# A two-layer graph network on one core: key one-hots on VectorE alone, elu read from PSUM, key sums by a block of ones

## The chip, the cores and the metric

The kernel runs on one core of one Trainium2 chip. The metric is the device time of one execution in microseconds. A core has TensorE (PE in the profile), VectorE (DVE), ScalarE (ACT), GpSimd (POOL) and SyncE (SP, which only issues transfers here). They run their own instruction streams and meet at semaphores.

## The reference, cut to what matters

Two layers on 1250 nodes of 512 features with 21250 weighted edges (`src`, `dst` sorted, `edge_weight`).

```python
xn = layernorm(x)
x = x + gcn(xn, edges, ew, W, b) + linear_attention(xn, w_qkv, w_out, b_out)
x = x + ffn0(layernorm(x))
xn = layernorm(x)
x = x + relu(segment_sum(((xn @ U * s) @ Vt)[dst] * ew, src) + bias) + softmax_attention(xn, w_qkv, w_proj, b_proj)
x = x + haar_ffn(layernorm(x))
# gcn: norm = dinv[row] * ew * dinv[col];  out[col] += (xn @ W)[row] * norm, self loops added
# linear_attention: q = elu(q) + 1, k = elu(k) + 1, 8 heads of 64;
#                   kv = k^T v, z = 1 / (q . sum_n k + 1e-6), out = (q kv) z
# softmax_attention: q = softmax(q, within a head), k = softmax(elu(k) + 1, over the nodes)
```

## The kernel before, in words

Nodes lie in T = 10 tiles of 128 rows (`nodes`). All products are made as three passes of fp32r halves: a tensor x is split into `hi` (rounded by ScalarE) and `lo` (the rest, by VectorE or GpSimd), and `THREE` names the pairs of halves that are multiplied.

**First layer, the pairs' stage** (54 to 206 us). The dense weighted adjacency `AT` (128 x 10 x 1280) is built from the edges. The edge list is 170 chunks of 128 edges, taken two by two: CP = 85 pairs. For a pair g the kernel needs `onehot` (128 edges x 128 source residues, for two chunks), `Loh` (that one-hot times the weight's two halves, 128 x 512, on GpSimd), and `Roh` (the key one-hot, 128 x 200, one for each chunk). `adj(g)` on TensorE multiplies `Loh` by `Roh` in four matmuls, and VectorE adds the result from PSUM into a window of `AT` (L1138). Before the change VectorE makes `onehot` as one bf16 operation (L1107) and the second `Roh` (L1109), while ScalarE makes the first `Roh` in two steps, |key - iota| (L514) and relu(1 - that) (L516). GpSimd waits for `oh_src`, which the `onehot` operation signals, and makes `Loh` (L858).

The pairs are interleaved with the products of the linear attention: for each tile t from 3 to 9, TensorE makes K and V of tile t, Q and H of tile t - 3 (`k_product` and so on, 4 blocks of three matmuls each) and `kv(t)`, and after each block as many `adj` as `pairs_by(blocks)` says. Three PSUM banks rotate over the products (`bank_of`); `evicted` names what must have read a bank before it is written again. The order on every engine is written out by hand: on VectorE `pairs_upto(n)` does, for each pair, the add into `AT` and then `onehots(g + 3)`, and between such runs stand `k_elu`, `xt_lo`, `k_lo`, `v_lo` and `q_elu`. elu(x) + 1 is min(exp(x), 1) + relu(x): ScalarE writes exp into `et` and relu into `rt`, both from PSUM, and VectorE combines the two SBUF tensors (`k_elu`, L1031; `q_elu`, L1044). `k_lo` (L1035) makes the low half of K. `block_of` and `slot_free` set how far an engine may run ahead (3 buffers of `Roh`, 4 of `Loh`).

**Ahead of the pairs** (to 54 us) the first tiles are normalised and multiplied, the weights are split (GpSimd's `split_lo`, one 128 x 2048 operation each for two weights, L844), and the edge keys are computed.

**Second layer, `keys`** (530 to 595 us). For each tile, TensorE adds khl2^T xn into four banks (12 matmuls, L1926) and the sum of the keys over the nodes with two columns of ones (8 small matmuls into `pKV[0]`, L1929). Between two tiles it transposes two blocks of `AT` (`turn_weights(k)`, L1890), which ScalarE and VectorE copy and split (`a2_hi`, `a2_lo`), and multiplies the block before by the low-rank features (`low_rank(k - 1)`, L1899 and L1900). Ahead of it, `kmax` (the maximum of the keys over all nodes) goes through a transpose, VectorE's L1409 and L1411, and a spreading matmul (L1915) to ScalarE's `kmaxb` (L743), which all keys wait for.

## Time and profile before

| | |
|---|---|
| median of 3 runs | 712.24 us |
| lowest, highest | 709.3, 723.59 us |
| the profiled execution: its own time | 716.19 us |
| the profiled execution: span | 714.4 us |
| mean granted TensorE clock | 0.921 |
| PE, DVE, ACT, POOL busy | 611.4, 500.3, 315.2, 246.1 us |

The span runs from the first to the last instruction; 1.8 us of the execution lie outside it. Busy times are sums over stages with different limits: TensorE is at 86% over the whole span, VectorE at 70%.

### The profile page before, as it was taken

The numbers are of one execution on the slowest core, as the hardware profiler recorded it, in microseconds if no ns is written. First come the engines' busy times: TensorE is split into PE (matmuls) and PEld (weight loads), VectorE is DVE, ScalarE is ACT, GpSimd is POOL, SyncE is SP. The second block draws the span as 40 slices with busy tenths as digits, with TensorE's granted clock in tenths as the row PEclk, the third lists the DMA queues.
The fourth block names the chain that finished last, engine by engine and source line by source line (L and its number), as shares of the span: only waits on it lengthen the run. The fifth ranks groups of instructions, "written<-read, shape, count | busy, mean of one in ns | idle before, by whom it ended". The sixth has DMA issues, their size and how long they took to land.

```text
span 714.4 us, 8713 instructions
## 1 busy us (share of the span) xinstructions
PE 611.4 (86%) x3024; PEld 488.4 (68%) x3024; DVE 500.3 (70%) x922; ACT 315.2 (44%) x601; POOL 246.1 (34%) x225
## 2 busy tenths in 40 slices
...
GB/s 322 71 2 0 1 2 1 2 0 1 1 2 60 59 30 18 28 83 11 60 125 1 0 1 0 1 0 0 74 0 1 1 0 1 75 0 1 0 1 144
DMA packets 15043, 21.10 MB, mean 30 GB/s; under 512 B 3260, under 2 KB 6000, under 8 KB 15002
## 3 DMA queue, kind: packets, MB, share of 16 engines
...
q14 instruction: 17, 0.14, 0.1%
...
## 4 chain that ended last, share of the span: by engine, by line
PE 69%; DVE 20%; ACT 5%; issue 4%; DVEq 1%; DMA 0%; ACTq 0%
PE p L1741 10%; PE p L1591 4%; PE pQ L1607 4%; PE pQ L1848 4%; PE p L1848 3%; PE pH L1607 3%; PE p L1823 2%; PE p L1926 2%; PE pH L1990 2%; PE pQ L1990 2%; PE pKV L1636 2%; DVE rt L1031 2%; PE p L1607 2%; PE pQ L1753 2%; PE pH L1753 2%
## 5 line engine op out<-in xcount | busy, mean ns | idle before, releaser
L858 POOL TENSOR_TENSOR Loh<-onehot,whl 128x512 fp32r<-128x512 bf16 x85 | 89.9, 1058 | 66.3 <-DVE onehot L1107 66.3
L1591 PEld LDWEIGHTS p<-Roh,Loh 128*128 128x128 f32 x340 | 49.2, 196 | 39.6 <-issue 34.7
L1741 PE MATMUL p<-G,ATs 128*128 128x512 f32 x300 | 71.3, 396 | 1.0 <-DVE G L1248 1.0
L1591 PE MATMUL p<-Roh,Loh 128*128 128x200 f32 x340 | 54.8, 284 | 19.1 <-DVE AT L1138 13.9
L1741 PEld LDWEIGHTS p<-G,ATs 128*128 128x128 f32 x300 | 57.4, 192 | 13.9 <-issue 1.8
L1107 DVE TENSOR_TENSOR onehot<-iota_src,srcb 128x256 bf16<-128x256 bf16 x85 | 65.8, 774 | 0.7 <-DVE flagint L1119 0.7
L971 POOL TENSOR_TENSOR xT<-xn,xT 128x512 fp32r<-128x512 f32 x10 | 12.9, 1291 | 134.2 <-ACT xT L707 134.1
L1607 PE MATMUL pQ<-wsl,xT 128*128 128x512 f32 x168 | 51.4, 438 | 3.1 <-DVE xT L1026 3.1
L514 ACT ACTIVATE away<-iota_key,key 128x200 f32<-128x200 f32 x85 | 38.9, 458 | 30.0 <-PE p L1591 29.8
L1607 PE MATMUL pH<-wsl,xT 128*128 128x512 f32 x168 | 46.4, 404 | 0.0
L873 POOL TENSOR_TENSOR ATs<-AT,ATs 128x1280 fp32r<-128x1280 f32 x10 | 29.9, 2996 | 35.8 <-ACT ATs L571 35.7
L516 ACT ACTIVATE Roh<-away,onesf 128x200 fp32r<-128x200 f32 x85 | 39.3, 463 | 2.8
L1607 PEld LDWEIGHTS pQ<-wsl,xT 128*128 128x128 f32 x168 | 32.8, 213 | 9.5 <-DVE xT L1026 4.0
L615 ACT ACTIVATE xT<-pT 128x512 fp32r<-128x512 f32 x10 | 6.0, 598 | 73.2 <-PE pT L1728 73.2
L1138 DVE TENSOR_TENSOR AT<-AT,p 128x200 f32 x85 | 30.0, 353 | 10.8 <-PE p L1591 6.1
L1848 PE MATMUL pQ<-Wq,xT 128*128 128x512 f32 x120 | 32.6, 424 | 1.8 <-DVE xT L1364 1.7
L1607 PE MATMUL p<-wsl,xT 128*128 128x512 f32 x120 | 33.3, 400 | 0.0
L1607 PEld LDWEIGHTS pH<-wsl,xT 128*128 128x128 f32 x168 | 29.8, 193 | 4.6
L1848 PE MATMUL p<-Wk,xT 128*128 128x512 f32 x120 | 30.0, 398 | 0.0
L1417 DVE TENSOR_TENSOR ATr<-pT,ATr 128x512 fp32r<-128x512 f32 (+1 forms) x15 | 9.0, 601 | 29.1 <-ACT ATr L723 29.1
L1848 PEld LDWEIGHTS pQ<-Wq,xT 128*128 128x128 f32 x120 | 23.4, 202 | 7.2 <-DVE xT L1364 2.4
L1109 DVE TENSOR_SCALAR Roh<-iota_key,key 128x200 fp32r<-128x200 f32 x85 | 27.3, 322 | 0.0
...
## 6 DMA issues: line engine op xcount, KB each, us to landing
...
```

The costliest lines, as they stand in the source:

```text
L514: act.activation(away[:, g % 2, :], iota_key[:], ACT.Abs, bias=key[:, 2 * g:2 * g + 1], scale=-1.0).then_inc(S["oh_y"], 1)
L516: act.activation(Roh[:, g % RSLOTS, 0, :], away[:, g % 2, :], ACT.Relu, bias=onesf[:, 0:1], scale=-1.0).then_inc(S["oh_act"], 1)
L858: pool.tensor_tensor(Loh[:, g % SLOTS], o, w, ALU.mult).then_inc(S["oh_pool"], 1)
L873: pool.tensor_tensor(ATs[:, t % 2, 1], AT[:, :, t * P:(t + 1) * P], ATs[:, t % 2, 0].bitcast(F32), ALU.subtract).then_inc(S["ats_lo"], 1)
L1107: v.tensor_tensor(onehot_[:, g % SLOTS], iota_src[:].rearrange("p (c n) -> p c n", c=1).broadcast_to([P, 2, P]), srcb[:, 2 * g:2 * g + 2]. ...
L1138: v.tensor_tensor(win, win, pW[g % 2][:, 0:T * WIN].rearrange("p (s w) -> p s w", s=T), ALU.add)\
L1591: ins = pe.matmul(pW[g % 2][:, 0:T * WIN], Loh[:, g % SLOTS, c, part, :], Roh[:, g % RSLOTS, c, :], start=(c + part == 0), stop=(c + part ...
L1607: ins = pe.matmul(bank[:, :], xT[:, t % XR, x, c, :], wsl[:, w, y, c, :], start=(c == 0 and n == 0), stop=(c == KC - 1 and n == 2))
L1741: ins = pe.matmul(pG[u][:, :], ATs[:, u, x, s_, :], G[:, y, s_, :], start=(s_ + n == 0), stop=(s_ == T - 1 and n == 2))
L1753: ins = pe.matmul(pM[u][:, :], xT[:, QT[u], x, c, :], WO[:, y, c, :], start=(c + n == 0), stop=(c == KC - 1 and n == 2))
L1848: ins = pe.matmul(o, xT[:, u, x, c, :], w[:, y, c, :], start=(c + n == 0), stop=(c == KC - 1 and n == 2))
L1990: pe.matmul(pM[u][:, :], xT[:, u, x, c, :], MW[:, y, c, :], start=(c + n == 0), stop=False)
```

## The change

Names as in the diff. (1) `onehots(g)`: VectorE makes `onehot` as two 128x128 fp32 comparisons, `oh_src` at the second, and both `Roh`; ScalarE's two steps and `away`, `srcb`, `oh_act` go. `onehot` is fp32r, so GpSimd reads fp32 where it read bf16. (2) elu(x) + 1 becomes max(x + 1, exp(-relu(-x))): ScalarE writes relu(-x) into `et` and then, after a wait on itself, exp(-et) over it; VectorE reads x from the PSUM bank. A bank of K or Q is then free after `k_elu` or `q_elu`. (3) `k_lo` of tiles 3 to 9 moves from VectorE to GpSimd, after `Loh` of the pair `pairs_by(block_of(t, 2)) + 2`, and `k_elu(t)` waits for `k_lo(t - 1)`. (4) `split_lo` becomes four 128 x 512 operations. (5) Ahead of the pairs, the layer norm of tiles 2 to 9 stands before `k_elu(0)` on VectorE and before `k_out(0)` on ScalarE. (6) In the second layer the key sums are two 512-column matmuls with a 128 x 128 block of ones (`onesr`), taken off the diagonal blocks on VectorE; `low_rank` lags `turn_weights` by two; the spreading matmul of `kmax` comes ahead of `low_rank(0)` and `turn_weights(2)`; the reciprocal of `sumq` moves behind the first `z_lo`.

```diff
             sp.wait_ge(S["e_dve"], 1)
             sp.wait_ge(S["rest_ok"], 1)
-            sp.wait_ge(S["oh_act"], CP)
+            sp.wait_ge(S["oh_pool"], CP)
             sp.wait_ge(S["q_elu"], T - LAG)
             sp.dma_start(raw[:], wview(a["L0_mix_w_out"])).then_inc(S["ld_wo"], 16)
...
                 if t >= 1:
-                    act.wait_ge(S["k_lo"], t)
-                act.activation(et[:], bank_of[WK, t][:, :], ACT.Exp).then_inc(S["k_er"], 1)
-                act.activation(rt[:], bank_of[WK, t][:, :], ACT.Relu).then_inc(S["k_er"], 1)
+                    act.wait_ge(S["k_elu"], t)
+                act.activation(et[:], bank_of[WK, t][:, :], ACT.Relu, scale=-1.0).then_inc(S["k_er"], 1)
+                act.wait_ge(S["k_er"], 2 * t + 1)
+                act.activation(et[:], et[:], ACT.Exp, scale=-1.0).then_inc(S["k_er"], 1)
...
             def h_out(t):
                 act.wait_ge(S["h_mm"], t + 1)
                 act.activation(nodes[:, t, :], bank_of[WH, t][:, :], ACT.Copy).then_inc(S["h_out"], 1)
-            made = [0]
-            def onehots_upto(blocks):
-                while made[0] < min(CP, pairs_by(blocks) + 2):
-                    g = made[0]
-                    made[0] += 1
-                    if g == 0:
-                        act.wait_ge(S["e_dve"], 1)
-                    slot_free(act, g)
-                    act.activation(away[:, g % 2, :], iota_key[:], ACT.Abs, bias=key[:, 2 * g:2 * g + 1], scale=-1.0).then_inc(S["oh_y"], 1)
-                    act.wait_ge(S["oh_y"], g + 1)
-                    act.activation(Roh[:, g % RSLOTS, 0, :], away[:, g % 2, :], ACT.Relu, bias=onesf[:, 0:1], scale=-1.0).then_inc(S["oh_act"], 1)
             ln_sqrt(1, 0, 2)
...
             normalise(1)
             split_hi(WV)
+            ln_sqrt(2, 2, T)
             k_out(0)
             act.wait_ge(S["e_pe"], 1)
             act.activation(rest[:, 0, :], pA[:, 2 * CH:3 * CH], ACT.Copy).then_inc(S["e_act"], 1)
             act.activation(rest[:, 1, :], pA[:, CH:2 * CH], ACT.Copy).then_inc(S["e_act"], 1)
             act.activation(srclo[:], pA[:, 0:CH], ACT.Copy).then_inc(S["e_act"], 1)
-            act.activation(srcb[:], pA[:, 0:CH], ACT.Copy).then_inc(S["e_act"], 1)
...
                 pool.wait_ge(S["w_hi"], i)
-                pool.tensor_tensor(wsl[:, i, 1], wraw[:, i, 1], wsl[:, i, 0].bitcast(F32), ALU.subtract).then_inc(S["w_lo"], 1)
+                for c in range(KC):
+                    ins = pool.tensor_tensor(wsl[:, i, 1, c], wraw[:, i, 1, c], wsl[:, i, 0, c].bitcast(F32), ALU.subtract)
+                ins.then_inc(S["w_lo"], 1)
+            def k_lo(t):
+                pool.wait_ge(S["k_hi"], t + 1)
+                pool.tensor_tensor(khl[:, 1, :], rt[:], khl[:, 0, :].bitcast(F32), ALU.subtract).then_inc(S["k_lo"], 1)
             pool.wait_ge(S["w_hi"], 1)
             for c in range(KC):
...
-                o = onehot_[:, g % SLOTS].rearrange("p c (k n) -> p c k n", k=1).broadcast_to([P, 2, 2, P])
+                o = onehot_[:, g % SLOTS].bitcast(F32).rearrange("p c (k n) -> p c k n", k=1).broadcast_to([P, 2, 2, P])
                 pool.tensor_tensor(Loh[:, g % SLOTS], o, w, ALU.mult).then_inc(S["oh_pool"], 1)
+                for t in range(LAG, T):
+                    if g == min(CP - 1, pairs_by(block_of(t, 2)) + 2):
+                        k_lo(t)
...
             def k_elu(t):
                 v.wait_ge(S["k_er"], 2 * t + 2)
-                v.scalar_tensor_tensor(rt[:], et[:], 1.0, rt[:], ALU.min, ALU.add).then_inc(S["k_elu"], 1)
+                if t >= 1:
+                    v.wait_ge(S["k_lo"], t)
+                v.scalar_tensor_tensor(rt[:], bank_of[WK, t][:, :], 1.0, et[:], ALU.add, ALU.max).then_inc(S["k_elu"], 1)
             def k_lo(t):
                 v.wait_ge(S["k_hi"], t + 1)
...
+            def q_elu(t, e=eq, bank=None):
                 v.wait_ge(S["q_er"], 2 * t + 2)
-                v.scalar_tensor_tensor(qbuf[:, t, :], e[:], 1.0, qbuf[:, t, :], ALU.min, ALU.add).then_inc(S["q_elu"], 1)
+                v.scalar_tensor_tensor(qbuf[:, t, :], (bank or bank_of[WQ, t])[:, :], 1.0, e[:], ALU.add, ALU.max).then_inc(S["q_elu"], 1)
             def stats(t0, t1):
...
-            k_elu(0)
-            xt_lo(1)
             v.wait_ge(S["ld_xc"], 16)
             step(stats(5, T))
             aggregate_stats(2, T)
             ln_coefficients(2, 2, T)
+            k_elu(0)
+            xt_lo(1)
             k_lo(0)
             v_lo(0)
...
             def onehots(g):
                 slot_free(v, g)
-                v.tensor_tensor(onehot_[:, g % SLOTS], iota_src[:].rearrange("p (c n) -> p c n", c=1).broadcast_to([P, 2, P]),
-                                srcb[:, 2 * g:2 * g + 2].rearrange("p (c n) -> p c n", n=1).broadcast_to([P, 2, P]), ALU.is_equal).then_inc(S["oh_src"], 1)
-                v.tensor_scalar(Roh[:, g % RSLOTS, 1, :], iota_key[:], key[:, 2 * g + 1:2 * g + 2], None,
-                                ALU.is_equal).then_inc(S["oh_dve"], 1)
+                for c in range(2):
+                    ins = v.tensor_scalar(onehot_[:, g % SLOTS, c, :], iota_src[:], srclo[:, 2 * g + c:2 * g + c + 1], None, ALU.is_equal)
+                ins.then_inc(S["oh_src"], 1)
+                for c in range(2):
+                    ins = v.tensor_scalar(Roh[:, g % RSLOTS, c, :], iota_key[:], key[:, 2 * g + c:2 * g + c + 1], None, ALU.is_equal)
+                ins.then_inc(S["oh_dve"], 1)
             def count_outside():
...
                 pairs_upto(pairs_by(block_of(t, 2)) + 1)
-                k_lo(t)
                 v_lo(t)
...
             tile1(T - 1, 1, last=True)
-            v.wait_ge(S["sq"], 2 * T)
...
             a2_lo(3)
+            v.wait_ge(S["sq"], 2 * T)
+            step(v.reciprocal(sumq[:], sumq[:]))
             for t in range(T):
                 u = t % 2
...
             v.tensor_tensor(Vt[:, 1, :], vraw[:], Vt[:, 0, :].bitcast(F32), ALU.subtract).then_inc(S["vt_lo"], 1)
-            v.wait_ge(S["z_mm"], T + after["z_mm"])
-            step(v.tensor_copy(ksum[:], pKV[0][:, 0:2 * PAIRS].rearrange("p (c n) -> p c n", n=2)[:, :, 0]))
+            v.wait_ge(S["z_one"], T + after["z_one"])
+            v.wait_ge(S["z_klo"], T + after["z_klo"])
+            diag = et[:].rearrange("p (c n) -> p c n", c=KC)
+            step(v.tensor_tensor(diag, pKV[0][:, :].rearrange("p (c n) -> p c n", c=KC),
+                                 ident[:].rearrange("p (c n) -> p c n", c=1).broadcast_to([P, KC, P]), ALU.mult))
+            step(v.tensor_reduce(ksum[:], diag, AX, ALU.add))
             v.reciprocal(ksum[:], ksum[:]).then_inc(S["zr_ok"], 1)
             v.wait_ge(S["zr_ok"], 1 + after["zr_ok"])
+            v.wait_ge(S["z_mm"], T + after["z_mm"])
             for b, (bank, o) in enumerate(((pH, et), (pQ, rt))):
                 v.tensor_scalar(o[:], bank[:, :], ksum[:, 2 + b:3 + b], None, ALU.mult).then_inc(S["zs_d"], 1)
             a2_lo(24)
...
             def adj(g):
                 pe.wait_ge(S["oh_dve"], g + 1)
-                pe.wait_ge(S["oh_act"], g + 1)
                 pe.wait_ge(S["oh_pool"], g + 1)
...
             pe.wait_ge(S["u_lo"], T)
-            low_rank(0)
-            turn_weights(2)
             pe.wait_ge(S["cm_ok"], 1 + after["cm_ok"])
             for p in range(PAIRS):
                 ins = pe.matmul(pH[:, p * P:(p + 1) * P], et[:, p * P:(p + 1) * P], ident[:], start=True, stop=True)
             ins.then_inc(S["cmb_ps"], 1)
+            turn_weights(2)
+            low_rank(0)
+            turn_weights(3)
             low_rank(1)
-            turn_weights(3)
-            low_rank(2)
             def keys(t, u, first=False, rows=P):
                 pe.wait_ge(S["z_xlo"], t + 1)
                 pe.wait_ge(S["z_klo"], t + 1 + after["z_klo"])
+                for x in range(2):
+                    ins = pe.matmul(pKV[0][:, :], onesr[0:rows, :], khl2[0:rows, u, x, :], start=(first and x == 0), stop=(rows < P and x == 1),
+                                    skip_group_check=True)
+                ins.then_inc(S["z_one"], 1)
                 for b, bank in enumerate(zbank):
                     for n, (x, y) in enumerate(THREE):
                         ins = pe.matmul(bank[:, :], khl2[0:rows, u, x, b * P:(b + 1) * P], xT[0:rows, u, y].rearrange("p c n -> p (c n)"),
                                         start=(first and n == 0), stop=(rows < P and n == 2), skip_group_check=True)
-                    for x in range(2):
-                        ins = pe.matmul(pKV[0][:, 2 * b:2 * b + 2], khl2[0:rows, u, x, b * P:(b + 1) * P], ones2[0:rows, :],
-                                        start=(first and b + x == 0), stop=(rows < P and x == 1), skip_group_check=True)
                 ins.then_inc(S["z_mm"], 1)
-            pe.wait_ge(S["c1"], 5)
+            pe.wait_ge(S["c1"], 6)
             for t in range(T):
...
                 keys(t, t % 2, t == 0, LAST if t == T - 1 else P)
                 for k in steps_at(t):
                     turn_weights(k)
-                    low_rank(k - 1)
+                    low_rank(k - 2)
             turn_weights(24)
+            low_rank(22)
+            turn_weights(25)
             low_rank(23)
-            turn_weights(25)
...
```

Not shown: `q_out` changes as `k_out` does; the first transfer of `raw` waits for `oh_pool` where it waited for `oh_act`; TensorE's waits on `q_er` in the tail of the first layer become waits on `q_elu`; `q_elu(6)` stands ahead of the reduction over `AT`; `onehots_upto` is gone from ScalarE's loop at all four places.

VectorE at the start of the first pairs: the first `AT` add, one `onehots`, and the steps of tile 3. Before:

```order
L1138 TENSOR_TENSOR AT<-AT,p 128x10x20
L1107 TENSOR_TENSOR onehot<-iota_src,srcb 128x256
L1109 TENSOR_SCALAR Roh<-iota_key,key 128x200
L1031 SCALAR_TENSOR_TENSOR rt<-et,rt 128x512
L1026 TENSOR_TENSOR xT<-pT,xT 128x512
L1138 ISA
L1138 TENSOR_TENSOR AT<-AT,p 128x10x20
```

and now:

```order
L1136 TENSOR_TENSOR AT<-AT,p 128x10x20
L1104 TENSOR_SCALAR onehot<-iota_src,srclo 128x128 x2
L1107 TENSOR_SCALAR Roh<-iota_key,key 128x200 x2
L1027 SCALAR_TENSOR_TENSOR rt<-pQ,et 128x512
L1020 TENSOR_TENSOR xT<-pT,xT 128x512
L1136 ISA
L1136 TENSOR_TENSOR AT<-AT,p 128x10x20
```

Where one onehot and one `Roh` stood between an `AT` add and `k_elu` there are two of each, and `k_elu` reads the bank `pQ`.

GpSimd from the weight splits to the end of the pairs. Before:

```order
L844 TENSOR_TENSOR wsl<-wraw,wsl 128x2048 x2
L858 TENSOR_TENSOR Loh<-onehot,whl 128x512 x85
L862 MEMSET xn 128x512
```

and now, up to tile 4:

```order
L829 TENSOR_TENSOR wsl<-wraw,wsl 128x512 x8
L848 TENSOR_TENSOR Loh<-onehot,whl 128x512 x6
L834 TENSOR_TENSOR khl<-rt,khl 128x512
L848 TENSOR_TENSOR Loh<-onehot,whl 128x512 x13
L834 TENSOR_TENSOR khl<-rt,khl 128x512
```

The split comes in eight pieces, and a `khl` (`k_lo`) stands after every 13 `Loh`.

TensorE in the second layer, from the low-rank product or the spreading matmul (pH<-ident,et) to the first `keys`. Before:

```order
L1899 MATMUL pKV<-ATr,uhl 128x512
L1900 MATMUL pKV<-ATr,uhl 64x512
L1890 MATMUL pT<-ident,AT 128x128 x4
L1915 MATMUL pH<-ident,et 128x128 x4
L1899 MATMUL pKV<-ATr,uhl 128x512
L1900 MATMUL pKV<-ATr,uhl 64x512
L1890 MATMUL p<-ident,AT 128x128 x4
L1899 MATMUL pKV<-ATr,uhl 128x512
L1900 MATMUL pKV<-ATr,uhl 64x512
L1926 MATMUL p<-xT,khl 128x512 x3
L1929 MATMUL pKV<-ones,khl 128x2 x2
L1926 MATMUL p<-xT,khl 128x512 x3
```

and now:

```order
L1914 MATMUL pH<-ident,et 128x128 x4
L1891 MATMUL pT<-ident,AT 128x128 x4
L1900 MATMUL pKV<-ATr,uhl 128x512
L1901 MATMUL pKV<-ATr,uhl 64x512
L1891 MATMUL p<-ident,AT 128x128 x4
L1900 MATMUL pKV<-ATr,uhl 128x512
L1901 MATMUL pKV<-ATr,uhl 64x512
L1925 MATMUL pKV<-khl,onesr 128x512 x2
L1930 MATMUL p<-xT,khl 128x512 x6
L1930 MATMUL pH<-xT,khl 128x512 x3
L1930 MATMUL pQ<-xT,khl 128x512 x3
```

The spreading matmul has moved ahead of a `turn_weights` and a `low_rank`, and `keys` begins with the two matmuls on `onesr`.

## Rows read from the trace of the kernel before

**Rows 1.** Windows, the pairs' stage: start:end, length, busy us of each engine.

```profile
54.46:206.50 152.04, 132.95 (x747) 105.97 (x746) 141.22 (x288) 103.25 (x223) 90.33 (x86) 0.98 0.00 1
```

**Rows 2.** Groups of instructions in 55 to 206 us: busy us, mean ns, idle before.

```profile
L858 POOL TENSOR_TENSOR Loh<-onehot,whl 128x512 fp32r<-128x512 bf16 x85 | 89.9, 1058 | 66.3 <-DVE onehot L1107 66.3
...
L1109 DVE TENSOR_SCALAR Roh<-iota_key,key 128x200 fp32r<-128x200 f32 x85 | 27.3, 322 | 0.0
...
L1031 DVE SCALAR_TENSOR_TENSOR rt<-et,rt 128x512 f32<-128x512 f32 x7 | 10.7, 1524 | 0.0
L1035 DVE TENSOR_TENSOR khl<-rt,khl 128x512 fp32r<-128x512 f32 x7 | 10.7, 1524 | 0.0
L1044 DVE SCALAR_TENSOR_TENSOR qbuf<-eq,qbuf 128x512 f32<-128x512 f32 x6 | 9.1, 1524 | 0.0
```

**Rows 3.** Timeline of VectorE, then of GpSimd, middle of the pairs' stage.

```profile
127.76 0.31 DVE L1109 TENSOR_SCALAR Roh<-iota_key,key 128x200 fp32r<-128x200 f32 x1
127.99 1.53 DVE L1031 SCALAR_TENSOR_TENSOR rt<-et,rt 128x512 f32<-128x512 f32 x1
129.44 0.68 DVE L1026 TENSOR_TENSOR xT<-pT,xT 128x512 fp32r<-128x512 f32 x1
...
130.31 0.41 DVE L1107 TENSOR_TENSOR onehot<-iota_src,srcb 128x256 bf16<-128x256 bf16 x1
130.65 0.31 DVE L1109 TENSOR_SCALAR Roh<-iota_key,key 128x200 fp32r<-128x200 f32 x1
130.88 0.35 DVE L1138 TENSOR_TENSOR AT<-AT,p 128x200 f32 x1
131.15 0.99 DVE L1107 TENSOR_TENSOR onehot<-iota_src,srcb 128x256 bf16<-128x256 bf16 x1
...
127.91 1.06 POOL L858 TENSOR_TENSOR Loh<-onehot,whl 128x512 fp32r<-128x512 bf16 x1 [0.36 <-DVE onehot L1107]
130.81 1.06 POOL L858 TENSOR_TENSOR Loh<-onehot,whl 128x512 fp32r<-128x512 bf16 x1 [1.83 <-DVE onehot L1107]
132.22 1.05 POOL L858 TENSOR_TENSOR Loh<-onehot,whl 128x512 fp32r<-128x512 bf16 x1 [0.36 <-DVE onehot L1107]
```

**Rows 4.** Where the first pairs are made: VectorE's timeline; `Loh`, ns min/median/max, first start.

```profile
55.37 1.10 DVE L1109 TENSOR_SCALAR Roh<-iota_key,key 128x200 fp32r<-128x200 f32 x1
...
L858 POOL TENSOR_TENSOR Loh<-onehot,whl x3: 1053/1056/1317, 55.0 to 57.7; 128x512 fp32r<-128x512 bf16 x3
```

**Rows 5.** Groups of instructions, 515 to 590 us: nearest rows to the new operations.

```profile
L971 POOL TENSOR_TENSOR xT<-xn,xT 128x512 fp32r<-128x512 f32 x10 | 12.9, 1291 | 134.2 <-ACT xT L707 134.1
...
L1411 DVE TENSOR_SCALAR et<-onesf,ksum 128x128 f32<-128x128 f32 x4 | 0.9, 281 | 0.0
```

**Rows 6.** Timeline of VectorE and GpSimd ahead of the pairs.

```profile
44.37 4.15 DVE L1031 SCALAR_TENSOR_TENSOR rt<-et,rt 128x512 f32<-128x512 f32 x1 [1.30 <-ACT rt L478]
...
43.38 4.59 POOL L844 TENSOR_TENSOR wsl<-wraw,wsl 128x2048 fp32r<-128x2048 f32 x1 [7.05 <-ACT wsl L454]
```

**Rows 7.** Windows of TensorE: the stage of `keys`; a stretch of pairs, the next.

```profile
530.37:588.69 58.32, 50.69 (x285) 1.00 0.00 1
...
87.80:91.20 3.40, 1.68 (x10) 0.99 0.01 2
91.20:94.60 3.40, 3.24 (x13) 0.51 0.03 7
```

**Rows 8.** Chain of work that ended last, second layer: start, us, what.

```profile
520.21 0.87 DVE et L1411 x4
...
523.87 1.72 PE pH L1915 x8
...
542.84 0.70 PE p L1926 x3
543.54 0.12 PE pKV L1929 x2
543.66 0.80 PE p L1926 x3
```

More of the change, by code:

```diff
@@ L183, in build @@
                     [("erow", [P, 3, 2, P], I32), ("frow", [P, 4, 2, P], F32)],
-                    [("edge", [P, 3, CH]), ("away", [P, 2, T * WIN]), ("eq", [P, D]), ("onehot", [P, SLOTS, 2, P], BF16)],
+                    [("edge", [P, 3, CH]), ("egap", [P, 2 * D - 3 * CH]), ("roomgap", [P, 2, T * WIN]), ("eq", [P, D])],
+                    [("onehot", [P, SLOTS, 2, P], F32R)],
                     [("raw", [P, KC, D], F32)],
@@ L189, in build @@
         erow, frow, edge, raw, xb, brow = (R1[n] for n in ("erow", "frow", "edge", "raw", "xb", "brow"))
-        away, eq, onehot_ = R1["away"], R1["eq"], R1["onehot"]
+        eq, onehot_ = R1["eq"], R1["onehot"]
         vraw, b2 = (R1[n] for n in ("vraw", "b2"))
@@ L334, in evicted @@
         def evicted(w, t):
-            return ((S["k_er"], 2 * t + 2), (S["v_lo"], t + 1), (S["q_er"], 2 * t + 2), (S["h_out"], t + 1))[w]
+            return S[("k_elu", "v_lo", "q_elu", "h_out")[w]], t + 1
         bank_of, freed = {}, {}
@@ L744, in _ @@
             zexp(0, 0, True)
+            zexp(1, 1, True)
             a2_hi(2)
-            zexp(1, 1, True)
             a2_hi(3)
@@ L764, in _ @@
             act.wait_ge(S["zr_ok"], 1 + after["zr_ok"])
+            act.wait_ge(S["z_mm"], T + after["z_mm"])
             for b, bank in enumerate((pK, pV)):
@@ L1204, in _ @@
             v.wait_ge(S["h_out"], T - 1 - LAG)
+            q_elu(T - 1 - LAG)
             v.tensor_reduce(pD, AT[:, 0:DEG_DVE, :].rearrange("p s d -> p d s"), AX, ALU.add).then_inc(S["degp_ok"], 1)
-            q_elu(T - 1 - LAG)
             v.wait_ge(S["degp_ok"], 1)
@@ L1212, in _ @@
             v.tensor_tensor(dhl[:, 1, :], pD, dhl[:, 0, :].bitcast(F32), ALU.subtract).then_inc(S["dhl_lo"], 1)
-            q_elu(T - 2, et)
-            q_elu(T - 1, et)
+            q_elu(T - 2, et, pKV[0])
+            q_elu(T - 1, et, pT)
             qs = [rt[:], xn[:, 1, :]]
@@ L1402, in _ @@
             tile1(T - 1, 1, last=True)
-            v.wait_ge(S["sq"], 2 * T)
-            step(v.reciprocal(sumq[:], sumq[:]))
             v.wait_ge(S["cm_ps"], 1 + after["cm_ps"])
@@ L1701, in _ @@
             pe.wait_ge(S["h_out"], T)
-            pe.wait_ge(S["q_er"], 2 * (T - 2))
+            pe.wait_ge(S["q_elu"], T - 2)
             for p in range(PAIRS):
```

45 lines of the change are left out of this document (20 added, 25 removed).

## The prediction

> **What bounds the kernel now.** I read the windows first, then the groups of instructions of the stage that the change rebuilds, then its timeline. In the pairs' stage (54.46 to 206.50 us, 152.0 us) VectorE is busy 141.2 us, TensorE 133.0, ScalarE 103.3 and GpSimd 90.3 [rows 1]. So VectorE is the tightest engine, but its busy time is not all work: `k_elu`, `k_lo` and `q_elu` (20 operations) take 1.524 us each [rows 2], and an `onehot` takes 0.99 us where another takes 0.41 [rows 3]. The timeline says why. `k_elu` starts at 127.99, GpSimd's `Loh` runs from 127.91 to 128.97, and `k_elu` ends at 129.52, 0.55 us after `Loh`; the onehot of 131.15 ends at 132.14, 0.27 us after the `Loh` of 130.81 [rows 3]. An operation with two SBUF inputs that is issued while `Loh` runs does nothing until `Loh` ends, and then ends after its own duration less 0.13 us. The `AT` add (one input in PSUM) takes 0.35 us beside the same `Loh` [rows 3]: it does not wait. The two engines therefore go in lockstep: `Loh` 1.05 us, then the end of the waiting onehot (0.27), then 0.08 to the next `Loh`, which is the idle 0.36 us on GpSimd [rows 3], 1.41 us a pair.
>
> That account adds up. 85 x 1.41 = 120 us. In each tile `k_elu` and `xt_lo` together, and `k_lo` and `v_lo` together, stretch GpSimd's idle time from 0.36 to 1.83 us [rows 3], so 1.47 more, and `q_elu` about 0.9 more: 7 x 1.47 + 7 x 1.47 + 6 x 0.9 - 0.6 (no `xt_lo` in the last tile) = 25. That is 145; the other 6.7 us of the stage are TensorE's waits and the loading of window registers, and I keep them.
>
> **ScalarE's two steps go: worth nothing here.** ScalarE is idle for 49 of the 152 us [rows 1], and it is not what VectorE waits for.
>
> **The one-hots: what each costs, and what they now wait for.** A 128x128 fp32 comparison with a scalar from SBUF is nearest to the 0.281 us of L1411 [rows 5]; operations start about 0.07 us before the one ahead ends (`Roh` of 0.31 us at 130.65, the next at 130.88) [rows 3], so 0.21 each, two of them 0.42 where the bf16 operation took 0.34. A second `Roh` adds 0.23. Alone that is 0.31 us a pair, 26 us in all. The question is whether the new operations wait for `Loh` too. They have one SBUF input, unlike those that wait above. Before the change a `Roh` always stands right behind the onehot that releases `Loh`, so it slips through at 0.31. Just one of the 85 was issued later: that of 55.37 took 1.10 us [rows 4]. The `Loh` beside it began at 55.03 and took 1.317 us, to 56.35; this `Roh` ended at 56.47, 0.12 after it [rows 4]. So a comparison waits too. The Trainium skill states the same as a rule (SBUF — State Buffer, "Who interferes with whom"): VectorE and GpSimd share one pair of SBUF ports, `tensor_scalar` in a two-port mode takes it, and whoever is issued second is blocked for the whole instruction. By that rule every new comparison contends; without it only the bf16 onehot did and the change would look like the cheap one; the trace agrees in its one instance.
>
> Now the order. `oh_src` is signalled at the second comparison. The first `Roh` is then already issued and passes. The second starts some 0.15 us after the signal, and `Loh` 0.08 us after it. That is exactly the place of `k_elu` in the old kernel (onehot, `Roh`, then `k_elu`), and there all 20 operations waited, without one exception [rows 2, 3]. So I take it that the second `Roh` waits for the whole of `Loh`, every time. From the end of `Loh`: the second `Roh` ends at 0.12, the `AT` add starts at 0.05 and takes 0.27, the two comparisons start at 0.32 and 0.53, the latter ends at 0.81, and the next `Loh` starts at 0.89. One pair costs `Loh` + 0.89 us.
>
> `Loh` itself: its onehot operand was bf16 (1.058 us [rows 2]) and is fp32 now. The nearest row by type and size is GpSimd's fp32 operation of 128x512, 1.291 us [rows 5]. Bounds 1.06 (the type does not matter) and 1.29; I take 1.29, since size, engine and both operand types are those. A pair: 2.18 us, 85 of them 185 us.
>
> **elu from PSUM and `k_lo` on GpSimd.** `k_elu` and `q_elu` have one SBUF input and stop waiting: 0.68 us, as L1026 from PSUM [rows 3], or 0.60 from start to start. With `xt_lo` and `v_lo` that makes 7 + 6 + 7 + 6 = 26 operations. They come after the blocked `Roh`, so when GpSimd is idle, and lie on the path in full: 15.6 us. `k_lo` leaves VectorE and costs GpSimd 1.29; behind it `Loh` is queued, and VectorE's comparisons wait for it; only the `AT` add and what else needs no port lies beside it. That is about 0.8 us on the path, 7 times: 5.6 us. The two dependent steps on ScalarE and the later release of the banks have cover: ScalarE has 49 us to spare in the stage already [rows 1].
> Stage: 185.3 + 15.6 + 5.6 + 6.7 = 213 us against 152: **+61 us**. At 1.06 for `Loh` it is +41.
>
> **Ahead of the pairs.** `k_elu(2)` waited 4.15 us, for GpSimd's weight split of 4.59 us [rows 6]; from PSUM it takes 0.7, so up to 3.4 us, less what is late next: the split now comes in pieces of 1.29 us, each of which can hold a later two-input operation. Against that the layer norm stands ahead of `k_elu(0)`; for it, two table loads fewer. Bounds 0 and -8; I take -5.
>
> **Second layer.** In `keys`, three matmuls take 0.70 us, 0.80 behind two small ones, which take 0.12 [rows 8]: 3.6 us a tile. Now 14 large matmuls at 0.233 are 3.27, so -0.3 a tile, -3. TensorE idles 58.3 - 50.7 = 7.6 us in this stage [rows 7], since `low_rank(k - 1)` waits for copies of a block just transposed; with a lag of two most of it goes: -7.5. The spreading matmul could begin at 521.1, when L1411 ends, and began at 523.87 [rows 8]: -2.8, and the reciprocal moved out of the way and the sums taken early are worth 2 to 3 more. Together -16, bounds -8 and -20.
>
> **Sum**: +61 - 5 - 16 = +40 us. The profiled execution took 716.2 us (span 714.4 and 1.8 outside it), so 756; it lies 4 us above the median of 712.2, and put against the median the forecast is **752 us**.
>
> **The rivals.**
> - *The second `Roh` passes before `Loh`.* It is a close race, 0.07 us. Then the wait moves to the next comparison, and the `AT` add and the tile's operations lie beside `Loh`. A pair: `Loh` + 0.75 = 2.04, 173 us; with 7 for `k_lo`, 1.4 for what sticks out and 6.7: 189, so +37 and 728 us. With the cheap `Loh` 708. For: nothing but the closeness; against: 20 of 20.
> - *`Loh` costs 1.06 with fp32 too*: 752 - 20 = 732 us.
> - *The clock.* TensorE would be busy 133 of 213 us. Behind a stretch in which TensorE was busy 1.68 of 3.4 us, the granted clock in the next was at its lower level, 1.2 GHz (0.51) [rows 7]. At that level a pair's work of 133/85 = 1.56 us becomes 3.1, more than the 2.18 of the pair. A quarter of the stage (53 us) at that level would hold 17 pairs in place of 24, so 16 us more: 768 us.
> - *Faster: one-input comparisons never wait.* Then the 1.10 us of [rows 4] had another cause. VectorE needs 85 x 1.15 + 15.6 + 6.7 = 120 us, GpSimd 85 x 1.37 + 9 = 125, and TensorE's 133 binds; with some waits 140, so -12 - 21: 679 us. It decides if the comparisons cost under some 0.7 us a pair with all their waits.
> - *The change does not do what it says*: ScalarE's part gone but VectorE still waiting on it; the diff leaves no such wait.
>
> **Chances.** As forecast 0.50; cheap `Loh` 0.15; second `Roh` passes 0.15; clock 0.10; no wait 0.05; the rest 0.05, for the first and second layer's own terms. The range leaves out the 679, the cheapest corner of the second rival and what lies beyond the clock: 718 to 768. Two per cent is about what a measurement here can tell from no change (698 to 726.5): faster 0.06, same 0.14, slower 0.80.
>
> **What would show it.** In the changed profile: `Roh` x170 in two kinds, 0.31 and about 1.4 us (mean some 0.85); `onehot` x170 at 0.28; `Loh` at 1.29 with 0.9 idle before most of them; `k_elu` and `q_elu` at 0.7; the stage some 213 us long with TensorE waiting for VectorE and GpSimd; `keys` shorter by about 1 us a tile. The forecast is wrong if `Roh` has a mean near 0.32 with onehots at 0.28, or if `Loh` stays at 1.06.

## The result, and the profile after

The changed kernel takes 722.95 us (median of 4 runs, 722.19 to 727.86) against 711.35 for the kernel before on the same chip (709.3 to 723.59): a ratio of 1.0192, with a 95% interval of 1.0141 to 1.0242. It is 10 to 17 us slower. The forecast was 752, 40 us slower: the sign was right, the time lies inside the range, and the size of the loss is less than half of what was forecast.

The windows of the pairs' stage and of `keys` after the change (start:end, length, busy us of PE, PEld, DVE, ACT, POOL, granted clock, DMA share, GB/s) stand beside [rows 1] and [rows 7]. The last two lines, after the change and before it, are what follows `keys` (from the start of its last tile to the transposes behind the layer's attention):

```profile
52.56:239.85 187.29, 145.83 (x747) 110.52 (x746) 184.68 (x451) 34.30 (x57) 98.83 (x93) 0.93 0.00 1
...
559.13:604.20 45.07, 45.07 (x230) 36.18 (x231) 25.01 (x38) 32.55 (x55) 10.35 (x8) 1.00 0.00 1
...
604.20:624.89 20.69, 16.39 (x116) 13.86 (x114) 10.85 (x21) 7.56 (x19) 0.53 (x1) 1.00 0.00 1
...
588.69:613.61 24.92, 22.34 (x121) 19.20 (x119) 8.46 (x18) 6.76 (x17) 0.53 (x1) 0.73 0.00 1
```

The pairs' stage has grown from 152.0 to 187.3 us, where +61 was forecast, and VectorE is busy for all but 2.6 us of it. The groups of the new operations, from the page of the changed kernel and its groups in 50 to 260 us:

```profile
L848 POOL TENSOR_TENSOR Loh<-onehot,whl 128x512 fp32r<-128x512 f32 x85 | 89.5, 1053 | 89.7 <-DVE onehot L1104 89.7
L1107 DVE TENSOR_SCALAR Roh<-iota_key,key 128x200 fp32r<-128x200 f32 x170 | 112.9, 704 | 0.0
...
L1104 DVE TENSOR_SCALAR onehot<-iota_src,srclo 128x128 fp32r<-128x128 f32 x170 | 46.2, 311 | 0.7 <-DVE flagint L1117 0.7
...
L834 POOL TENSOR_TENSOR khl<-rt,khl 128x512 fp32r<-128x512 f32 x7 | 9.1, 1299 | 0.0
```

Against [rows 2]: `Loh` takes 1.053 us with fp32 operands, as it took 1.058 with a bf16 one. `k_lo` on GpSimd has the same size and takes 1.299. VectorE's timeline, then GpSimd's, in the middle of the stage (equal neighbours are put together, x2):

```profile
125.86 0.35 DVE L1136 TENSOR_TENSOR AT<-AT,p 128x200 f32 x1
126.14 0.47 DVE L1104 TENSOR_SCALAR onehot<-iota_src,srclo 128x128 fp32r<-128x128 f32 x2
126.53 1.33 DVE L1107 TENSOR_SCALAR Roh<-iota_key,key 128x200 fp32r<-128x200 f32 x2
127.78 0.35 DVE L1136 TENSOR_TENSOR AT<-AT,p 128x200 f32 x1
...
126.68 1.05 POOL L848 TENSOR_TENSOR Loh<-onehot,whl 128x512 fp32r<-128x512 f32 x1 [0.86 <-DVE onehot L1104]
128.60 1.05 POOL L848 TENSOR_TENSOR Loh<-onehot,whl 128x512 fp32r<-128x512 f32 x1 [0.86 <-DVE onehot L1104]
```

Two comparisons of a `Roh` one behind the other would take 0.54 us (0.31, and 0.23 from start to start [rows 3]); here they take 1.33 and end 0.13 us after `Loh`. The second `Roh` took over 0.9 us in 84 of the 85 pairs, the first never over 0.33. The chain of work that ended last has a piece of 1.25 us for 62 of the pairs (start, us, what):

```profile
56.33 1.25 DVE Roh L1107 x2
58.25 1.25 DVE Roh L1107 x2
```

A pair costs 1.92 us: `Loh` 1.05 + 0.87, where before it was 1.41. The forecast's own signs say the same: the wait came (GpSimd idle 0.86 us ahead of `Loh`, forecast 0.9), and "`Loh` stays at 1.06", which it named as a sign of being wrong, came too.

The rest of the program, by TensorE's timeline. The last pair's matmuls start at 238.72 (205.67 before, +33.1); a late product of the second layer's Q starts at 527.93 (495.16, +32.8); the transposes behind the end of the layer's attention at 624.89 (613.61, +11.3). So 21.5 us come back in `keys` and what lies around it: 3.8 between the last products of Q and `keys` (21.3 to 17.5 us), 13.4 in `keys` (58.5 to 45.1) and 4.2 behind it (24.9 to 20.7). The two waits of TensorE ahead of and behind `keys`:

```profile
553.53 2.05 PE L1914 MATMUL pH<-ident,et 128*128 128x128 f32 x8 [2.92 <-DVE et L1406]
...
612.85 0.41 PE L1949 MATMUL p<-ident,xn 128*128 128x128 f32 x2 [2.98 <-DVE rt L1464]
```

By these executions the whole is +6.7 us (spans 721.1 and 714.4). The profiled execution of before was itself 4.8 us above its median; the windows show where a part of that may lie: TensorE's granted clock was 0.73 in 588.69 to 613.61 (24.9 us), and 1.00 in the same stretch after the change (604.20 to 624.89, 20.7 us). Medians and experiments decide below, not that pair of traces alone.

### The profile page after: what moved, and what is told of

It is laid out like the page before. It is cut to its first block, busy times and chain, and to the rows that moved or that the text cites. A ratio compares the mean times of both kernels' runs of the same rounds, so it can differ in the third digit from the quotient of the medians.

```text
span 721.1 us, 8526 instructions
## 1 busy us (share of the span) xinstructions
PE 602.1 (83%) x2964; PEld 474.7 (66%) x2964; DVE 543.9 (75%) x1086; ACT 242.5 (34%) x428; POOL 253.8 (35%) x239
## 4 chain that ended last, share of the span: by engine, by line
PE 59%; DVE 34%; ACT 3%; issue 3%; DVEq 1%; DMA 0%; ACTq 0%
DVE Roh L1107 13%; PE p L1742 10%; PE pQ L1849 4%; DVE onehot L1104 4%; PE p L1849 3%; DVE AT L1136 3%; PE p L1824 2%; PE pH L1992 2%; PE p L1930 2%; PE pH L1608 2%; PE pQ L1992 2%; PE p L1608 2%; PE pQ L1608 2%; PE pH L1754 2%; PE pQ L1754 2%
## 5 line engine op out<-in xcount | busy, mean ns | idle before, releaser
L848 POOL TENSOR_TENSOR Loh<-onehot,whl 128x512 fp32r<-128x512 f32 x85 | 89.5, 1053 | 89.7 <-DVE onehot L1104 89.7
L1107 DVE TENSOR_SCALAR Roh<-iota_key,key 128x200 fp32r<-128x200 f32 x170 | 112.9, 704 | 0.0
L1592 PE MATMUL p<-Roh,Loh 128*128 128x200 f32 x340 | 59.1, 299 | 39.9 <-DVE AT L1136 38.7
L1608 PE MATMUL pH<-wsl,xT 128*128 128x512 f32 x168 | 48.3, 417 | 0.0
L1104 DVE TENSOR_SCALAR onehot<-iota_src,srclo 128x128 fp32r<-128x128 f32 x170 | 46.2, 311 | 0.7 <-DVE flagint L1117 0.7
L1608 PE MATMUL p<-wsl,xT 128*128 128x512 f32 x120 | 39.0, 456 | 5.0 <-DVE xT L1020 5.0
L1608 PEld LDWEIGHTS p<-wsl,xT 128*128 128x128 f32 x120 | 24.5, 225 | 9.2 <-DVE xT L1020 5.4
L982 POOL TENSOR_SCALAR nodes<-nodes,small,nmr 128x512 f32<-128x512 f32 x10 | 10.6, 1070 | 47.6 <-DVE sn L1524 47.6
L1849 PEld LDWEIGHTS p<-Wk,xT 128*128 128x128 f32 x120 | 21.9, 188 | 4.2
## 6 DMA issues: line engine op xcount, KB each, us to landing
wraw<-in_L_mix_w_qkv SPq DMA_DIRECT2D x1, 1024.0 KB, 11.3
```

The lines of the kernel that those rows point to most:

```text
L848: pool.tensor_tensor(Loh[:, g % SLOTS], o, w, ALU.mult).then_inc(S["oh_pool"], 1)
L1104: ins = v.tensor_scalar(onehot_[:, g % SLOTS, c, :], iota_src[:], srclo[:, 2 * g + c:2 * g + c + 1], None, ALU.is_equal)
L1107: ins = v.tensor_scalar(Roh[:, g % RSLOTS, c, :], iota_key[:], key[:, 2 * g + c:2 * g + c + 1], None, ALU.is_equal)
L1592: ins = pe.matmul(pW[g % 2][:, 0:T * WIN], Loh[:, g % SLOTS, c, part, :], Roh[:, g % RSLOTS, c, :], start=(c + part == 0), stop=(c + part ...
L1608: ins = pe.matmul(bank[:, :], xT[:, t % XR, x, c, :], wsl[:, w, y, c, :], start=(c == 0 and n == 0), stop=(c == KC - 1 and n == 2))
L1849: ins = pe.matmul(o, xT[:, u, x, c, :], w[:, y, c, :], start=(c + n == 0), stop=(c == KC - 1 and n == 2))
```

## The experiments

**e1, the pairs' part alone.** The kernel before with the one-hots of the change and nothing else.

```diff
-    v.tensor_tensor(onehot_[g], iota_src, srcb[2g:2g+2], ALU.is_equal).then_inc(S["oh_src"], 1)
-    v.tensor_scalar(Roh[g, 1], iota_key, key[2g+1], None, ALU.is_equal)     # the other Roh on ScalarE
+    for c in range(2): ins = v.tensor_scalar(onehot_[g, c], iota_src, srclo[2g+c], None, ALU.is_equal)
+    ins.then_inc(S["oh_src"], 1)
+    for c in range(2): v.tensor_scalar(Roh[g, c], iota_key, key[2g+c], None, ALU.is_equal)
```

> The kernel before with only the pairs' part of the change: two fp32 comparisons for the one-hot and two for `Roh`, all on VectorE, ScalarE without part; the elus, `k_lo`, the preparation and the second layer stay as before. Theory: the whole loss lies in the pairs' stage and comes from the second `Roh`, which waits for `Loh` each time. A pair then takes `Loh` 1.05 + 0.86 = 1.91 us, 162 us for 85, and 33 tile operations of 0.60 (20 us) plus some 5 us of waits make 187 to 190 us for a stage of 152: +35 to +38, so about 747 us. `k_elu`, `k_lo` and `q_elu` should fall from 1.52 to 0.69 us, since they now come when GpSimd is idle. Rival: a good part of the +35 seen in the changed kernel came from `k_lo` on GpSimd; then this kernel is at +20 or less, 731 us.

Measured: 753.54 us against 710.53, ratio 1.0597 (1.0547 to 1.0647), so +43; by the spans of the two profiled executions 748.0 against 714.4, +33.6. Its stage, from the windows:

```profile
51.00:240.00 189.00, 152.03 (x751) 118.31 (x752) 183.96 (x460) 32.51 (x57) 89.87 (x86) 0.89 0.00 1
```

The first one-hot starts at 51.7 and the last add ends at 240.0: 188 us; the second `Roh` waits in all 85 pairs; and the elus, `k_lo` and `q_elu` took 0.68 each. Both as the theory had it. The pairs' part alone carries the loss, all of it and more. The time is 6 us above what I expected, and 9 of the 43 us are not in the pair of traces: e1's profiled execution was its fastest of five (749.76), that of before one of its slower ones. TensorE's granted clock was 0.90 over this execution against 0.92 in before; whether that is the reason no run shows.

**e2, the second layer's part alone.**

```diff
...
+    for x in range(2): pe.matmul(pKV[0], onesr, khl2[u, x], ...)            # ahead of the tile's 12
-        for x in range(2): pe.matmul(pKV[0][:, 2b:2b+2], khl2[u, x, b], ones2, ...)
...
-    low_rank(k - 1)
+    low_rank(k - 2)
...
```

> The kernel before with only the second layer's part (key sums by a block of ones, summed before the main matmuls of a tile; low-rank products two steps behind; order of the exponentials; reciprocal moved). Theory: this part alone gives what the changed kernel won back between TensorE's 528 and 613 us, 21 us: about 690 us, 0.970 of before. Rival: that win was partly slack made by the late start or by the clock, and alone the part gives the 16 us of the forecast or less: 695 us or more.

Measured: 696.25 us, ratio 0.9769 (0.9713 to 0.9825), so 12 to 20 us faster: the 16 us of the forecast. By spans it is 19.3, near the 21.5 of the traces. The rival (695 or more) fits better than my theory (690, at the edge of the interval, 690 to 698). Some 5 of the 21.5 us are clock: the stretch behind `keys` took 24.9 us at a granted clock of 0.73 in before, 19.9 at 1.00 in f4 (below), where TensorE does as many matmuls (121). Whether that clock belongs to the one execution or to the old order is open: e1, the only other kept trace with the old second layer, has 0.66 there, those with the new one 0.85 to 1.00.

**e3, the signal to GpSimd one comparison later.**

```diff
-                ins.then_inc(S["oh_src"], 1)             # at the second one-hot
-                for c in range(2):
-                    ins = v.tensor_scalar(Roh[..c..], ...)
+                v.tensor_scalar(Roh[.., 0, :], ...).then_inc(S["oh_src"], 1)
+                v.tensor_scalar(Roh[.., 1, :], ...).then_inc(S["oh_dve"], 1)
```

> The changed kernel with one edit: `Loh` is released by the first `Roh` comparison of its pair in place of the second one-hot comparison. Theory (whatever of VectorE's SBUF-only work is issued while `Loh` runs waits for its end; what is issued before passes): the second `Roh` is issued before `Loh` and takes 0.31, the wait moves to the first one-hot comparison, and the `AT` add and the tiles' operations from PSUM lie beside `Loh`. A pair takes 1.05 + 0.73 = 1.78 us, and the 26 tile operations (15.6 us) cost little: stage 187 to 165, so about 700 us. Rival (the two engines slow each other down by sharing memory, in whatever order): mean of `Roh` stays near 0.7 and the time at 721 to 725 us, since `Loh` starts 0.2 us later.

Measured: 696.48 us, ratio to before 0.9789 (0.9729 to 0.985), and 26 us under the changed kernel. The timelines:

```profile
123.16 0.31 DVE L1106 TENSOR_SCALAR Roh<-iota_key,key 128x200 fp32r<-128x200 f32 x1
123.39 0.35 DVE L1134 TENSOR_TENSOR AT<-AT,p 128x200 f32 x1
123.67 0.98 DVE L1104 TENSOR_SCALAR onehot<-iota_src,srclo 128x128 fp32r<-128x128 f32 x2
124.57 0.31 DVE L1105 TENSOR_SCALAR Roh<-iota_key,key 128x200 fp32r<-128x200 f32 x1
124.80 0.31 DVE L1106 TENSOR_SCALAR Roh<-iota_key,key 128x200 fp32r<-128x200 f32 x1
...
123.32 1.05 POOL L848 TENSOR_TENSOR Loh<-onehot,whl 128x512 fp32r<-128x512 f32 x1 [0.59 <-DVE Roh L1105]
124.96 1.05 POOL L848 TENSOR_TENSOR Loh<-onehot,whl 128x512 fp32r<-128x512 f32 x1 [0.59 <-DVE Roh L1105]
```

The second `Roh` is issued 0.16 us before `Loh` and takes 0.31; no `Roh` of the 170 took over 0.33 us. The wait is now the first one-hot's (mean 0.65 us, 0.35 before this edit). The instructions are the same, with the same memory traffic; only which of them is behind `Loh` in time has changed. Mutual slowing in whatever order is out. A pair takes 1.64 us; I expected 1.78, having counted the way from the end of `Loh` to the next one 0.14 too long (the first one-hot ends 0.10 after `Loh`, the second at 0.28, the first `Roh` at 0.51, the next `Loh` starts at 0.59).

**e4, the ramps in PSUM.**

```diff
+            for bank in pW:
+                step(v.tensor_copy(bank[:, T * WIN:2 * T * WIN], iota_key[:]))
-    v.tensor_scalar(Roh[..c..], iota_key[:], ...)
+    v.tensor_scalar(Roh[..c..], ikeys[(g + 1) % 2], ...)                   # one-hots likewise
-                pe.wait_ge(S["oh_dve"], g + 1)
+                pe.wait_ge(S["oh_dve"], min(CP, g + 2))
```

> The changed kernel with the ramps that the comparisons read (iota) held in PSUM, in the free columns of the two banks of the window sums; TensorE waits for the one-hots of the pair after as well, so that it never writes a bank that VectorE reads. Number and order of the instructions are the same. Theory: an operation with its input in PSUM does not wait for GpSimd, so all four comparisons run beside `Loh`: `Roh` has a mean near 0.3 us, VectorE needs 85 x 1.15 + 15.6 = 113 us and TensorE, 133, becomes the bound: stage 187 to about 150, time about 684 us. Rival one: the wait has to do with the SBUF write, not the read; `Roh` stays at 0.7, time 721. Rival two: the added wait of TensorE takes the gain, stage 165 or more.

Measured: 691.81 us, ratio 0.971 (0.9638 to 0.9782). From the page:

```profile
L848 POOL TENSOR_TENSOR Loh<-onehot,whl 128x512 fp32r<-128x512 f32 x85 | 88.4, 1040 | 61.1 <-DVE onehot L1106 60.9
...
L1109 DVE TENSOR_SCALAR Roh<-p,key 128x200 fp32r<-128x200 f32 x170 | 63.6, 415 | 0.0
...
L1106 DVE TENSOR_SCALAR onehot<-p,srclo 128x128 fp32r<-128x128 f32 x170 | 51.2, 342 | 0.0
```

No comparison waits any more (`Roh` 0.410 to 0.420 us, all 170), though each still writes SBUF and 205 of the 340 start while a GpSimd operation runs. So what makes a comparison wait is that its tensor input lies in SBUF, not that it writes there. By the Trainium skill (SBUF — State Buffer, "Who interferes with whom"), an instruction of VectorE with one SBUF input stays on its own ports outside the two-port modes, and in such a mode it and GpSimd shut each other out, the later one waiting for the whole of the earlier. The traces agree: the `AT` add, with one of its two inputs in SBUF, takes 0.35 us beside `Loh`, and in e3 the comparison issued second waits for all of it. They also fit a faster mode that is used from SBUF alone: from 128 to 200 columns a comparison grows by 0.036 us from SBUF (0.275 to 0.311) and by 0.073 from PSUM (0.342 to 0.415). The stage is 154.6 us, not 150: from PSUM a comparison costs 0.07 and 0.10 us more, so VectorE needs 1.46 us a pair, 85 x 1.46 + 15.6 = 140, where I had put 113.

The last pair shows that it is not the read alone. Behind its `Loh` GpSimd sets a tile to zero (a memset, which reads nothing). After the change (first three lines) the second `Roh` waits for that too and ends 0.12 us behind it, as in e1 and f3; in f2 it got in ahead, and the memset took 0.64 us in place of 0.52. In before (last two) `k_lo`, with two SBUF inputs, stands beside the same memset and ends 0.55 us after `Loh`, as it always does:

```profile
236.07 1.05 POOL L848 TENSOR_TENSOR Loh<-onehot,whl 128x512 fp32r<-128x512 f32 x1 [0.36 <-DVE onehot L1104]
237.07 0.52 POOL L855 MEMSET xn<- 128x512 f32 x1
235.91 1.79 DVE L1107 TENSOR_SCALAR Roh<-iota_key,key 128x200 fp32r<-128x200 f32 x2
...
204.05 0.52 POOL L862 MEMSET xn<- 128x512 f32 x1
203.13 1.52 DVE L1035 TENSOR_TENSOR khl<-rt,khl 128x512 fp32r<-128x512 f32 x1
```

So an operation with two SBUF inputs did not wait for an instruction that only writes, and a comparison from SBUF did. It is one place in each kernel.

**f1, all of the change but its pairs' part.** The reverse of e1.

> The changed kernel with the pairs' part taken back: the bf16 one-hot on VectorE, one `Roh` by ScalarE and one by VectorE, as before; elu from PSUM, `k_lo` on GpSimd, the order of the preparation and the second layer as changed. Theory (the new comparisons are the whole loss; once VectorE no longer sets the pace, TensorE does, and its stage cannot fall much under the 152 to 155 us of the kernel before and of the kernel with its ramps in PSUM): stage 148 to 154, time 688 to 694 us. Rival: the elu part is worth much by itself, since 20 operations of 1.52 us fall to 0.68: then the stage falls by up to 17 us, to 135, and the time to 677 us.

Measured: 681.2 us, ratio 0.9562 (0.9484 to 0.9641): the fastest kernel of the study, 31 us under before. Its stage, and `Loh` and the bf16 one-hot on its page:

```profile
52.90:193.75 140.85, 130.10 (x747) 105.37 (x746) 126.05 (x280) 104.23 (x223) 100.08 (x93) 0.99 0.00 1
```

```profile
L868 POOL TENSOR_TENSOR Loh<-onehot,whl 128x512 fp32r<-128x512 bf16 x85 | 89.9, 1058 | 43.7 <-DVE onehot L1123 43.7
...
L1123 DVE TENSOR_TENSOR onehot<-iota_src,srcb 128x256 bf16<-128x256 bf16 x85 | 64.4, 758 | 0.7 <-DVE flagint L1135 0.7
```

Here my theory fell and the rival held for the most part. From the first one-hot to the last add the stage is 141 us, 11 shorter than before; GpSimd's idle time ahead of `Loh` has gone from 66.3 [rows 2] to 43.7 us, since `k_elu` and `q_elu` run beside `Loh`. I had taken 152 for TensorE's floor because before and e4 both stood there; in each TensorE stood mostly for VectorE (13.9 us for the `AT` add in before, 16.9 us for `Roh` in e4). Now TensorE, busy 130 of 141, comes nearest to setting the pace.

The parts do not simply add. With the old comparisons the elu part (with `k_lo`'s move) is worth 11 us of the stage (152.0 to 140.9). With the new ones it is worth 0.9 (187.8 in e1 to 187.0 after the change), since there the old elus, issued when GpSimd is idle, did not wait either. And against f1 the new comparisons cost the stage 46 us, the whole kernel 42.

**f2 and f3, the price of `Loh`.**

```diff
f2:  Loh    ALU.mult -> ALU.subtract;          k_lo   ALU.subtract -> ALU.mult
f3:  Loh    second operand whl (each value repeated 128 times in a row) -> wsl[:, WV, 1, 0] (512 stored values)
     k_lo   second operand khl[:, 0, :] (512 stored values)    -> khl[:, 0, 0:1] repeated 512 times
```

> The changed kernel with the operations of two GpSimd instructions exchanged: `Loh` subtracts in place of multiplying, `k_lo` multiplies in place of subtracting. The sizes and access patterns are kept; the adjacency and the keys come out as other numbers. It is to tell why `Loh` took 1.05 us where I priced it by 1.29. If the operation sets the price, `Loh` goes to 1.30 and `k_lo` to 1.05; if the form of the operands does, both stay as they are.

> The changed kernel with the operand forms of the same two instructions changed: the second operand of `Loh` is 512 stored values in place of four repeated 128 times each, and the second operand of `k_lo` is one value repeated 512 times in place of 512 stored ones. The adjacency and the keys come out as other numbers. If the operand's form sets the price, `Loh` goes from 1.05 to about 1.30 and `k_lo` from 1.30 to about 1.05, and the pairs' stage grows by 85 x 0.25 = 21 us, which is the term of the forecast that was too high; if it does not, both stay.

One execution each. Groups of GpSimd in f2, then in f3:

```profile
L848 POOL TENSOR_TENSOR Loh<-onehot,whl 128x512 fp32r<-128x512 f32 x85 | 89.7, 1055 | 89.9 <-DVE onehot L1104 89.9
...
L834 POOL TENSOR_TENSOR khl<-rt,khl 128x512 fp32r<-128x512 f32 x7 | 9.1, 1297 | 0.0
```

```profile
L849 POOL TENSOR_TENSOR Loh<-onehot,wsl 128x512 fp32r<-128x512 f32 x85 | 110.3, 1297 | 92.3 <-DVE onehot L1105 92.3
L834 POOL TENSOR_TENSOR khl<-rt,khl 128x512 fp32r<-128x512 f32 x7 | 7.4, 1058 | 0.0
```

The operation makes no difference; the form of the second operand makes all of it, both ways. With stored values `Loh` costs the 1.29 of my forecast and the last add starts at 261.8 instead of 239.5: 22 us, the term that was too high.

**f4, the lag and the order of the spreading matmul alone.**

```diff
-            low_rank(0)
-            turn_weights(2)
             pe.wait_ge(S["cm_ok"], 1 + after["cm_ok"])
...
+            turn_weights(2)
+            low_rank(0)
+            turn_weights(3)
...
-                    low_rank(k - 1)
+                    low_rank(k - 2)
...
```

> The kernel before with only one step of the second layer's part: the low-rank products stand two blocks behind the transposes in place of one, and the matmul that spreads the key maxima stands ahead of the first of them. Theory: TensorE's idle 7.6 us in the stage of `keys` go, and the spreading matmul starts 2.8 us sooner: -10 of the -16 us, ratio about 0.986. Rival: the key sums by 28 small matmuls were what cost; then this is worth 3 us or less and the other half, which has the sums by a block of ones and the earlier sums and exponentials, carries the gain.

Measured: 696.86 us, ratio 0.979 (0.9714 to 0.9865), as much as the whole second-layer part. The windows of `keys` in f4 (start of the first to start of the last tile) and of what follows it:

```profile
525.23:574.07 48.84, 48.84 (x285) 40.99 (x286) 24.34 (x37) 32.48 (x55) 10.34 (x8) 1.00 0.00 1
574.07:593.96 19.89, 16.85 (x121) 14.40 (x120) 9.63 (x20) 7.58 (x19) 0.53 (x1) 1.00 0.01 1
```

TensorE's idle 7.6 us are all gone [rows 7], and 2 us of busy time with them, for the same matmuls: `keys` is 9.6 us shorter than before, and 3.4 more come from what lies ahead of it (17.9 us since the last products of Q, 21.3 before), where the spreading matmul now follows L1411 within 0.2 us. The block of ones and the earlier sums take another 3.8 us out of `keys` (45.1 in the changed kernel) and 0.4 ahead of it, and give 0.8 back behind it: that stretch takes 20.7 us in the changed kernel and 19.9 in f4, both at a granted clock of 1.00. There VectorE must take the sums off the diagonal (a product and a reduction of 512 columns, 0.68 and 0.69 us) while TensorE waits, 2.98 us against 1.74. By the traces that half is therefore worth some 3.4 us; the times of e2 and f4 (696.25 and 696.86) can't tell the two kernels apart.

**g1, f1 with `k_lo` on VectorE again.**

> The kernel of f1 (everything of the change but its pairs' part) with `k_lo` taken back from GpSimd to VectorE. It is to split the 14 us that the elu part gained in the pairs' stage. Theory: what is worth the most is that `k_elu` and `q_elu` no longer wait for `Loh` (13 operations, 1.52 to 0.68, and GpSimd's gap behind each). `k_lo` has two SBUF inputs and waits again (1.52 us, 7 times) and stretches GpSimd's gap by about 0.9 each: the stage is 4 to 7 us longer than in f1 (146 to 149), the time 685 to 688. Rival: `k_lo` on GpSimd (1.3 to 1.5 us, 7 times) costs there what it saves, and the time stays at 681.

Measured: 686.38 us (679.57 to 690.09), ratio 0.9586 (0.9428 to 0.9744). That interval holds f1's, so the time decides nothing. In the trace `k_lo` waits again (1.524 us, 7 times) and the stage is 143.2 us against 140.9: 2.4 us, less than expected. Of the 11 us of f1's stage, the elus from PSUM carry about 9.

**g2, e3 with the added wait of e4.**

> The kernel of e3 (`Loh` released by the first `Roh` comparison) with the one wait that e4 added: TensorE waits for the comparisons of the pair after as well. It tells what that wait costs, since e4 came out at 692 us where I expected 684. TensorE stood 16.9 us before pairs' matmuls for VectorE's comparisons in e4. Theory: the wait is what kept e4 from TensorE's own pace; put on e3 it costs up to as much, 5 to 15 us, so 702 to 711. Rival: the comparisons from PSUM are slower (0.42 and 0.34 us against 0.31 and 0.28), and that took the gain; then the wait costs nothing here and the time stays at 696 to 698.

Measured: 697.69 us (695.85 to 700.12) against e3's 696.48. The ratio's interval (0.9684 to 0.9904, up to 703 us) is too wide to shut out the low end of my theory; the trace decides. The stage is 160.1 us against e3's 157.2, so here the wait costs some 3 us, under the 5 to 15 of the theory. The dearer reads from PSUM, counted above, are then the larger part of what kept e4 at 692. TensorE's 16.9 us of waits in e4 had read like a cost of the wait, but were for the most part the time that VectorE needs in any case.

## Why the prediction was wrong, step by step

**The failed term** is the price of `Loh`: "since size, engine and both operand types are those" I took 1.29 us from [rows 5]. It measured 1.053. 85 x 0.24 = 20 us of the 26 us by which the stage was over-priced. Size, engine and types were the same; the operation was not (a subtraction in [rows 5], a multiplication in `Loh`), but f2 shows that it makes no difference. What I did not compare was the access: the row of [rows 5] reads 512 stored values from each operand, `Loh` repeats each value of its weights 128 times. f3 turns either price into the other. The kernel before had the better row in hand: its own `Loh` with the same repeated weights, 1.058 [rows 2], differing only in one operand's type. I had it as the lower bound and as a rival with a chance of 0.15, at 732 us. It should have been the forecast. That 722.95 lies inside the range all the same is owed to the range, drawn down to 718 to hold this rival (732) and the one in which the second `Roh` passes (728), and not to the sum.

**Right, and shown:** that the second `Roh` waits for the whole of `Loh`, in 84 of 85 pairs (in all 85 of e1), from one instance in 85 [rows 4] and the place of `k_elu`. The pair was priced at `Loh` + 0.89 and took `Loh` + 0.87. e3 and e4 show that the issue while `Loh` runs, and the input in SBUF, are what count. The rival in which it passes gave 2.04 a pair, `Loh` + 0.75; forced by the signal in e3 it was `Loh` + 0.59, and the kernel then is faster than before, not slower.

**Smaller errors in the stage.** With the right `Loh` the forecast was +41; the measured +35. Of the 6 us, 2 lie in the pair (1.92 against 1.94), 4 in the waits and register loads that I had kept at 6.7 and `k_lo` at 5.6: 187.3 - 85 x 1.92 - 15.6 = 8.5 us for both. Against e1 the elu part and `k_lo`'s move brought next to nothing (0.9 us). The 15.6 for the operations from PSUM rests on their 0.60 in a place where GpSimd is idle, as the timeline after shows.

**Ahead of the pairs:** -5 forecast, -1.9 measured (the first one-hot at 52.56 instead of 54.46). `k_elu(2)` did fall from 4.15 to 0.69 us, but starts 0.39 later and a `k_lo` behind it waits 1.1 for a piece of the split: the "less what is late next" was underrated.

**Second layer:** -16 forecast; -12 to -20 by e2. The size is right. By the traces the lag and the spreading matmul, put at -7.5 and -2.8, brought 9.6 us in `keys` and 3.4 ahead of it (f4); the sums by a block of ones and the reordering beside them, put at -3 and another -2 to -3, brought 3.4 in all.

**ScalarE's part gone: nothing.** e1's stage came out as summed without it, so nothing speaks against it while VectorE sets the pace; no run takes it out alone. **The clock:** 0.93 in the stage; TensorE's busy time there rose from 133 to 146 us, with no visible price, since it still had 41 us to spare.

Sum with the measured terms: +35 - 2 - 16 = +17 us, at the upper end of the 10 to 17 that were measured. The medians differ by 11.6; the 5 us between, no run here assigns.
